# Probabilities transposed by DMA instead of TensorE, and second-half query columns multiplied tile by tile

## The reference

```
x = x + attn(layernorm(x));  x = x + ffn(layernorm(x))

qkv = (x @ w_qkv.T).reshape(B, N, 3, H, hd);  q, k, v = ...
att = softmax(einsum('bnid,bnjd->bnij', q, k) * hd**-0.5)   # over the 16 heads of one token
out = einsum('bnij,bnjd->bnid', att, v)
attn = out.transpose(0, 2, 1, 3).reshape(B, N, D) @ w_proj.T

ffn = fake_quant(relu(fake_quant(x) @ fake_quant(kernel) + fake_quant(bias)))
```

## Time and profile before

| | |
|---|---|
| three runs, us | 636.46, 634.66, 635.04; median 635.04 |
| the profiled execution, us | 635.95, with a span of 634.3 from first to last instruction |
| cores in it | 631.6 to 634.3 us, granted clock 0.990 to 0.993 |
| TensorE busy | 606.1 us (96%) |
| VectorE, ScalarE, GpSimd busy | 407.9 us (64%), 266.6 us (42%), 34.7 us (5%) |
| DMA | 103.48 MB, mean 163 GB/s |

### The profile page before, as it was taken

The page is one execution under the profiler, slowest core; times in us unless marked ns, Lnnn a source line. Parts: engine busy times, 40 slices in busy tenths (PEclk is TensorE's granted clock), DMA queues, the critical chain, the costliest instruction groups (busy, mean ns, idle before and its releaser), DMA issues.

```text
span 634.3 us, 9870 instructions; the slowest of 8 cores (631.6 to 634.3 us)
## 1 busy us (share of the span) xinstructions
PE 606.1 (96%) x3468; PEld 304.6 (48%) x3468; DVE 407.9 (64%) x685; ACT 266.6 (42%) x491; POOL 34.7 (5%) x68
## 2 busy tenths in 40 slices
PE   6768999999999999999999999999999999999993
PEld 6634444444444444444444455555555444444442
DVE  3745888777778768761001346787787654888557
ACT  2763333443333344330010465767877422653331
POOL 0000100000100100001120000000000000000000
PEclk9999999999999999999999999999999999999998
DMA  8997899889999999758996672384433494062313
GB/s 236 261 217 221 139 237 219 174 190 195 190 230 185 228 232 194 177 102 150 154 157 102 120 168 78 101 246 121 133 94 61 157 285 136 30 196 106 102 66 133
DMA packets 54114, 103.48 MB, mean 163 GB/s; under 512 B 35633, under 2 KB 35633, under 8 KB 50225
## 3 DMA queue, kind: packets, MB, share of 16 engines
q0 software_dynamic: 9216, 33.56, 33.4%
q1 hardware_dynamic: 42674, 60.90, 31.7%
q10 hardware_dynamic: 2176, 8.39, 3.9%
HBM read 111.21 MB, written 16.79 MB: 202 GB/s over the span
## 4 chain that ended last, share of the span: by engine, by line
PE 89%; DMA 6%; DVE 2%; issue 1%; SPq 1%; ACT 1%; DVEq 0%; ACTq 0%
PE pF L832 50%; PE pF L937 17%; PE pF L914 17%; DMA xbuf<-x_att 6%; PE pF L871 1%; PE pF L895 1%; PE pH L881 1%; PE pF L872 1%; SPq L219 1%; PE pF L956 1%; PE pF L850 1%; DVE cols L514 0%; DVE xr L640 0%; DVEq L214 0%; DVE xr L807 0%
## 5 line engine op out<-in xcount | busy, mean ns | idle before, releaser
L832 PE MATMUL pF<-aT,wqb 128*128 128x512 bf16 x1504 | 327.1, 379 | 5.0 <-DMA wqb<-wqkv 5.0
L832 PEld LDWEIGHTS pF<-aT,wqb 128*128 128x128 bf16 x1504 | 146.4, 98 | 179.3 <-issue 5.4
L914 PE MATMUL pF<-wpq,qT 128*128 128x512 bf16 x512 | 119.6, 379 | 0.0
L937 PE MATMUL pF<-kq,xqT 128*128 128x512 bf16 x496 | 107.2, 379 | 1.2 <-DVE xr L640 1.2
L937 PEld LDWEIGHTS pF<-kq,xqT 128*128 128x128 bf16 x496 | 48.5, 98 | 59.9 <-issue 1.7
L914 PEld LDWEIGHTS pF<-wpq,qT 128*128 128x128 bf16 x512 | 47.8, 98 | 47.2
L385 ACT ACTIVATE wkz<-wkf 128x2048 f32<-128x2048 f32 x16 | 59.1, 3691 | 21.0 <-DVE wkf L607 21.0
L395 ACT ACTIVATE Ebuf<-pF,cols 128x128 bf16<-128x128 f32 x128 | 45.4, 368 | 24.6 <-DVE cols L621 24.5
L541 DVE CAST vT<-pF 128x512 bf16<-128x512 f32 x16 | 11.0, 689 | 62.7 <-PE pF L832 62.7
L685 DVE SCALAR_TENSOR_TENSOR tt<-pF,cols,bqb 128x512 f32<-128x512 f32 x31 | 23.2, 749 | 33.0 <-PE pF L937 33.0
L320 POOL DMA_DIRECT2D wqb<-wqkv x48 | 26.0, 543 | 298.7 <-PE pF L832 244.0
(11 more groups left out here) (79 smaller groups left out, 533.4 us busy)
## 6 DMA issues: line engine op xcount, KB each, us to landing
wqb<-wqkv POOLq DMA_DIRECT2D x48, 512.0 KB, 8.1
wkf<-wk SPq DMA_DIRECT2D x16, 1024.0 KB, 8.4
xbuf<-x_att SPq DMA_DIRECT2D x8, 1024.0 KB, 19.9
kq_spill<-kqr SPq DMA_DIRECT2D x16, 512.0 KB, 5.9
wpq<-wp POOLq DMA_DIRECT2D x16, 512.0 KB, 9.6
xr<-x_res ACTq DMA_DIRECT2D x8, 1024.0 KB, 6.7
kq<-kq_spill SPq DMA_DIRECT2D x4, 2048.0 KB, 11.1
out<-xr SPq DMA_DIRECT2D x7, 1024.0 KB, 4.2
```

The lines of the kernel that those rows point to most:

```text
L832: mm = tn.matmul(pF[QBANK[j]][:, :], wqb[e % NW][:, 128 * c:128 * (c + 1)], aT[:, 8192 * h + 512 * c: 8192 * h + 512 * (c + 1)], start=(c ...
L914: mm = tn.matmul(pF[SLOTB[f % 3]][:, :], sT[:, 2048 * b + 128 * m: 2048 * b + 128 * (m + 1)], wpq[u][:, 512 * m:512 * (m + 1)], start=(m = ...
L937: mm = tn.matmul(pF[y % 4][:, :], xqT[:, 2048 * k + 128 * c: 2048 * k + 128 * (c + 1)], w[:, c, :, :], start=(c == 0), stop=(c == NC - 1))
```

## The change

The transposes of the probabilities leave TensorE and become DMA transposes on SP's queue (`e_transpose`), from `Ebuf` straight to `aTT`, so ScalarE's copy goes as well. `Ebuf` and `aTT` get three buffers each. SP's fixed list is built anew around the 32 transposes: V tile b goes after group 4b-2's transpose, the load of `kq[0]` after group 8's, layer-norm transposes 0 to 2 after groups 17, 23 and 29. In the head the second half of jobs 4 to 7 is done token tile by token tile, over the four jobs, with the transposes of tiles 5 to 7 between; tile 4's transpose comes after job 1, and none between jobs 2 and 3. Weight blocks 1 to 3 are given out one token tile earlier. SP's first FFN loads wait for the seventh normalised tile instead of job 3. ScalarE alternates strictly between normalising a tile and copying its transpose, and VectorE copies job 2 ahead of tile 6's statistics. The zeros for the warm-up matmuls get a name of their own.

```diff
--- before.py
+++ after.py
@@ -92,9 +92,10 @@
     wqb = [A(f"wqb{i}", [128, 2048], BF16, offset=180224 + 4096 * i)
            for i in range(NW)]
     Ebuf = [A(f"Ebuf{i}", [128, 512], BF16, offset=204800 + 1024 * i)
-            for i in range(2)]
-    aTT = [A(f"aTT{i}", [128, 512], BF16, offset=206848 + 1024 * i)
-           for i in range(2)]
+            for i in range(3)]
+    aTT = [A(f"aTT{i}", [128, 512], BF16, offset=207872 + 1024 * i)
+           for i in range(3)]
+    zero = A("zero", [128, 128], BF16, offset=204800)
     ident = A("ident", [128, 128], BF16, offset=210944)
     neg = A("neg", [128, 128], BF16, offset=211200)
     cols = A("cols", [128, 312], F32, offset=211456)
@@ -223,7 +224,7 @@
                     inc(sync.dma_start(ident[:, :], d_ident[:, :]), "cL", 16)
             inc(sync.dma_start(neg[:, :], d_neg[:, :]), "cN", 16)
 
-            sync.wait_ge(S_("qMM"), 4)
+            sync.wait_ge(S_("aN"), 7)
             inc(sync.dma_start(wkf[0][:, :], d_wk[0:128, :]), "kL0", 16)
             inc(sync.dma_start(wkf[1][:, :], d_wk[128:256, :]), "kL1", 16)
             sync.wait_ge(S_("qMM"), 5)
@@ -257,6 +258,15 @@
                     V8[b % 2].rearrange("p (c n) -> p c n", c=NC),
                     vT[:, 2048 * b:2048 * (b + 1)]), f"vT{b}", 16)
 
+            def e_transpose(g):
+
+                sync.wait_ge(S_("vNm"), g + 1)
+                if g >= 3:
+                    sync.wait_ge(S_("tO"), g - 2)
+                inc(sync.dma_start_transpose(
+                    aTT[g % 3].rearrange("p (j n) -> p j n", j=4),
+                    Ebuf[g % 3][:, :]), f"eT{g % 3}", 16)
+
             def l_transpose(b):
                 sync.wait_ge(S_("lQ"), 2 * b + 2)
                 inc(sync.dma_start_transpose(
@@ -279,15 +289,16 @@
                     d_out[128 * k:128 * (k + 1), :].rearrange(
                         "p (h c) -> p h c", h=2), xr_tile(k)), "oS", 16)
 
-            for b in range(5):
-                v_transpose(b)
-            kq_load(0)
-            l_transpose(0)
-            v_transpose(5)
-            v_transpose(6)
-            l_transpose(1)
-            v_transpose(7)
-            l_transpose(2)
+            v_transpose(0)
+            v_transpose(1)
+            for g in range(NG):
+                e_transpose(g)
+                if g % 4 == 2 and 2 <= g // 4 + 1 < NT:
+                    v_transpose(g // 4 + 1)
+                if g == 8:
+                    kq_load(0)
+                if g in (17, 23, 29):
+                    l_transpose((g - 17) // 6)
             sync.wait_ge(S_("tO"), NG)
             sync.wait_ge(S_("bSt"), 16)
             inc(sync.dma_start(bqb[:, :], d_bq.partition_broadcast(128)),
@@ -329,7 +340,7 @@
 
             for e in range(NE):
                 if e < 5:
-                    g.wait_ge(S_(f"xL{e + 2 if e else 1}"), 16)
+                    g.wait_ge(S_(f"xL{(1, 2, 3, 4, 6)[e]}"), 16)
                 if e >= NW:
                     g.wait_ge(S_("qMM"), JIDX[(e - NW, 1)] + 1)
                 wq_load(e)
@@ -388,11 +399,11 @@
 
             def exps(g):
                 s.wait_ge(S_("vMx"), g + 1)
-                if g >= 2:
-                    s.wait_ge(S_("tA"), g - 1)
+                if g >= 3:
+                    s.wait_ge(S_(f"eT{g % 3}"), 16 * (g // 3))
                 for j in range(4):
                     cs = slice(128 * j, 128 * (j + 1))
-                    i = s.activation(Ebuf[g % 2][:, cs], pF[3 + g % 2][:, cs],
+                    i = s.activation(Ebuf[g % 3][:, cs], pF[3 + g % 2][:, cs],
                                      AF.Exp, bias=cc(C_NM[g % 2] + j),
                                      accum_out=cc(C_DEN[g % 2] + j))
                 inc(i, "sEx")
@@ -404,12 +415,6 @@
                 inc(s.dma_start(
                     xr_tile(b), d_xres[128 * b:128 * (b + 1), :].rearrange(
                         "p (h c) -> p h c", h=2)), f"xrL{b}", 16)
-
-            def att_evac(g):
-                s.wait_ge(S_("tA"), g + 1)
-                if g >= 2:
-                    s.wait_ge(S_("tO"), g - 1)
-                inc(s.copy(aTT[g % 2][:, :], pH[g % 2][:, 0:512]), "sAT")
 
             def st_evac(g):
                 s.wait_ge(S_("tO"), g + 1)
@@ -454,17 +459,11 @@
             at_evac(0)
             norm(2)
             at_evac(1)
-            norm(3)
-            at_evac(3)
-            norm(4)
-            norm(5)
-            at_evac(4)
-            q_evac(1)
-            norm(6)
-            at_evac(5)
-            norm(7)
-            at_evac(6)
-            at_evac(7)
+            for t in range(3, NT):
+                norm(t)
+                at_evac(t)
+                if t == 4:
+                    q_evac(1)
             for j in range(3, NQ):
                 if j % 2 == 1:
                     q_evac(j)
@@ -480,8 +479,6 @@
                     exps(sl)
                 if sl < NG and sl % 4 == 3:
                     xres_load(sl // 4)
-                if 1 <= sl and sl - 1 < NG:
-                    att_evac(sl - 1)
                 b, r = (sl - L0) // LP, (sl - L0) % LP
                 if 0 <= b < NT:
                     if r < 2:
@@ -628,7 +625,7 @@
                 h = inc(v.reciprocal(cc(C_RD[g % 2], 4), cc(C_DEN[g % 2], 4)),
                         "vS")
                 wt(v, h)
-                e3 = Ebuf[g % 2].rearrange("p (j n) -> p j n", j=4)
+                e3 = Ebuf[g % 3].rearrange("p (j n) -> p j n", j=4)
                 rb = cc(C_RD[g % 2], 4).unsqueeze(2).broadcast_to([128, 4, 128])
                 inc(v.tensor_tensor(e3, e3, rb, ALU.mult), "vNm")
 
@@ -701,7 +698,7 @@
 
             inc(v.memset(cc(C_EPS), EPS), "aVar0")
             inc(v.memset(cc(C_NMG), -MAGIC), "vNmg")
-            inc(v.memset(aTT[0][:, 0:128], 0.0), "vZ")
+            inc(v.memset(zero[:, :], 0.0), "vZ")
             stats(0)
             stats(1)
             at_evac(0)
@@ -711,13 +708,13 @@
             at_evac(2, both=True)
             stats(4)
             at_evac(3)
-            stats(5)
             q_evac(0)
             at_evac(4)
+            stats(5)
+            q_evac(2)
             stats(6)
+            at_evac(5)
             stats(7)
-            at_evac(5)
-            q_evac(2)
             at_evac(6)
             at_evac(7)
             for j in range(4, NQ):
@@ -873,18 +870,8 @@
                                    start=False, stop=True)
                 inc(mm, "tS")
 
-            def a_transp(g):
-                tn.wait_ge(S_("vNm"), g + 1)
-                if g >= 2:
-                    tn.wait_ge(S_("sAT"), g - 1)
-                for j in range(4):
-                    tr = tn.transpose(pH[g % 2][:, 128 * j:128 * (j + 1)],
-                                      Ebuf[g % 2][:, 128 * j:128 * (j + 1)],
-                                      ident[:, :])
-                inc(tr, "tA")
-
             def av(g):
-                tn.wait_ge(S_("sAT"), g + 1)
+                tn.wait_ge(S_(f"eT{g % 3}"), 16 * (g // 3 + 1))
                 if g % 4 == 0:
                     tn.wait_ge(S_(f"vT{g // 4}"), 16)
                 if g >= 1:
@@ -894,7 +881,7 @@
                     c0 = 512 * (g % 4) + 128 * j
                     mm = tn.matmul(pF[2][:, cs],
                                    V8[(g // 4) % 2][:, c0:c0 + 128],
-                                   aTT[g % 2][:, cs], start=True, stop=True)
+                                   aTT[g % 3][:, cs], start=True, stop=True)
                 inc(mm, "tO")
 
             def p_part(b, u, c0, c1):
@@ -963,8 +950,8 @@
             def warm(n):
 
                 for i in range(n):
-                    tn.matmul(pF[5][:, 0:128], aTT[0][:, 0:128],
-                              aTT[0][:, 0:128], start=True, stop=True)
+                    tn.matmul(pF[5][:, 0:128], zero[:, :],
+                              zero[:, :], start=True, stop=True)
 
             tn.wait_ge(S_("vZ"), 1)
             warm(144)
@@ -977,13 +964,17 @@
             a_transpose(3)
             q_tiles(0, 0, 3, 12, NC)
             q_tiles(0, 3, 4)
-            for j in range(1, 4):
-                q_part(j, 0, NC)
-                a_transpose(3 + j)
-            a_transpose(7)
-            q_tiles(4, 0, 3)
-            q_tiles(4, 3, 4)
-            for j in range(5, NQ):
+            q_part(1, 0, NC)
+            a_transpose(4)
+            q_part(2, 0, NC)
+            q_part(3, 0, NC)
+
+            for t in range(4):
+                for e in range(HEADE):
+                    q_tiles(HEADE + e, t, t + 1)
+                    if e == 1 and t < 3:
+                        a_transpose(5 + t)
+            for j in range(2 * HEADE, NQ):
                 q_part(j, 0, NC)
 
             for sl in range(NS):
@@ -999,8 +990,6 @@
                         y_part(*YORD[sl - Y0], c0, c1)
                     elif half == 0:
                         y_last()
-                    if half == 0 and 1 <= sl <= NG:
-                        a_transp(sl - 1)
```

## The result

| | before | changed |
|---|---|---|
| runs, us | 634.66 to 636.46, median 635.11 (4) | 645.84, 648.46, 641.73, 648.49, median 647.15 |
| ratio | | 1.0164, 95% interval 1.0108 to 1.022 |
| the profiled execution | 635.95 (span 634.3) | 645.84 (span 644.2) |

The change made the kernel 1.6% slower; 628.9 was forecast, in 625 to 633. Each ratio is to the kernel before as timed beside that run (median 634.48 to 635.38 in the experiments); it is not the quotient of two medians.

The account below looks back on a forecast made before the run. The prediction took TensorE as the bound, with 89% of the chain of waits. 635.95 - 7.0 (attention) + 0.5 (stall) + 0.3 (head) = 629.75, less 0.9 for the median: 628.9 us, range 625 to 633.

Parts of the forecast that it names:

- Four transposes less per slot, -7.0: Attention: 32 slots each lose 0.22 us of TensorE transposes, 7.0 us in all, so a slot becomes 4.13.
- A landing of 2.3 us: Attention: each 128x512 DMA transpose lands in 2.3 us (bounds 1.8 and 5.3), hidden in the 6.9 to 8.2 available.
- transposes set the pace: Attention rival: with three buffers, landings above 8.8 us make slots longer than before; 648 at 10 us; chance 0.09.
- The 2 MB load, +0.5: Attention: the first FFN weight load holds group 9's transpose behind it on SP's queue; stall 0 to 0.8, taken as 0.5.
- the forecast's worst case: Attention: the stall from the 2 MB load with the next V transpose in between, 3 us at worst.
- Head, +0.3: Head: the whole rearrangement, with jobs 4 to 7 tile by tile, comes out 0.3 us slower.
- Job 3's wait: Head: TensorE's idle time before job 3 grows from 2.07 to 3.1 us.
- both waits on ScalarE: Head: TensorE waits 0.9 and 0.8 us for ScalarE's chain before the transposes of tiles 6 and 7.
- The clock: Head rival: the new 3.1 us gap brings the half clock, 3.5 us of it lose 1.7, giving 630.6; chance 0.15.
- Weights bound by shared DMA time: Head: issuing blocks 1 to 3 earlier lengthens the queue, not the rate; block 3 still arrives at 46.2.
- VectorE's lag hidden: After the head: VectorE's later FFN weight work is done at 91.1, before job 15 needs the bank at 92.9.
- The stated signs for "wrong": Slot above 4.13, TensorE idle before most attention products, PSUM-copy waits near job 15, clock 0.5 after 46, job 3 ending well before 49.

Follow-up runs that it names:

- e6: As e3, but the last quarter of the output projection's weights and the eight residual loads are constant fills instead of loads; 631.48 us, ratio 0.9942.
- e4: As e3, but the second V transpose is issued after group 1's transpose instead of before group 0's; 674.52 us, ratio 1.0599.
- e3: The changed kernel with the head of before and the first FFN weight quarter's load issued after the 32nd transpose; 649.5 us, ratio 1.0248.
- e1: The kernel before with only the head of the changed one, attention as before; 637.67 us, ratio 1.0044.
- e12: As e1, but weight blocks 1 to 3 are issued at the old token tiles; 636.69 us, ratio 1.0034.
- e9: As e3, but residual loads on SP's queue, groups 0 to 5 transposed by TensorE, kq[0] in four pieces, second layer-norm transpose after group 24; 629.6 us, ratio 0.9916.

## Why the prediction was wrong

- **Four transposes less per slot, -7.0: right.** Slot 4.12; e6 shows -6.8 in all.
- **A landing of 2.3 us: right alone, wrong in company.** This is the step that failed. It was scaled from V transposes that had the DMA engines to themselves (78% of a slice on one queue), with 5.3 as the upper bound; the changed kernel showed up to 15.3, e4 up to 33.4. Of the 32 new ones many must run beside GpSimd's weight loads (slots 1 to 4) and the residual loads (every fourth slot). The forecast counted the bytes of this traffic as nothing and never asked who else was on the DMA engines when a transpose runs. The rival "transposes set the pace" had the sign and the size (648), but named no cause and got 0.09; its condition, a landing over 8.8 us, held for a few transposes and not for all, so the loss comes in two or three large waits and not in every slot. That its number fits is luck.
- **The 2 MB load, +0.5: right for group 9, too small in all.** The stall before group 9's product came, 1.45 us on the slowest core, 0.95 and 0.45 on two others, none on five. With the 7.26 before group 11's, which the forecast's worst case put at 3, the waits before groups 9 to 11 come to 10.1 us over the eight cores. e3 takes such waits away and gains nothing, since those at the residual loads grow.
- **Head, +0.3: the waits right, the base wrong.** Job 3's wait and both waits on ScalarE came within 0.2 us of the forecast; job 8's start did too, but only since an earlier block 3 and the half clock cancel. A piece is 55.8 ns (96 of them from 63.48 to 68.84), near the 55 that the prediction states, though its own numbers, 1.05 less 0.2 over sixteen, give 53. And the forecast was set against core 5, the slowest of the profile before, whose job 8 began at 68.3; the mean over the cores was 66.5 (start of job 5 plus 10.35), against 68.4 in the changed kernel. The head costs 1.8 by that, 2.7 by e1's time.
- **The clock: it did fall,** on five of eight cores, the rival given 0.15. Its premise, that a gap of 2.1 us leaves the pace alone, was read on core 5; in the same profile job 2 of core 0 took 5.30 us after a gap of 2.04. The time is that of the slowest core, so a loss of 1.7 us on some cores can count in full: the slowest core of the changed kernel and that of e1 both have it.
- **Weights bound by shared DMA time: right** (e12). **VectorE's lag hidden: right,** no wait in jobs 8 to 89.
- The stated signs for "wrong" named TensorE idle before the attention product in most slots. It was idle before four of the 32 on the slowest core, three times for more than 1 us, and that was enough.

## What to carry to other kernels

Before work moves from an idle-free engine to DMA, list for each new transfer what other queues have in flight at that moment, not only whether its own queue is free: here transposing DMAs alone landed in 2.3 us, and the slowest beside other queues in 10 to 33. If they must be there, put everything that moves at the same time into the transposes' own queue, in order, and leave to TensorE those that would meet a queue you can't move (e9). Take the base of a forecast from all cores, since the slowest core before needn't be the slowest after.

## What the runs showed of the hardware that was not expected

- A 128x512 bfloat16 DMA transpose needs 0.58 us of the DMA engines alone (544 packets) and 1.2 us of SP's queue to issue. Beside one other queue 534 packets took 4 us (changed kernel, core 6); beside two, 976 took 20 us at 53 GB/s in sum over all queues (e4, core 6), plain transfers included.
- Giving a V transpose a later place in the same queue cost 25 us (e4 against e3), by what it then met.
- The clock: in the changed kernel gaps of 2.30 to 2.99 us before job 3 were followed by the half clock on five cores (5.07 to 5.30 us for the job), gaps of 2.09, 2.43 and 3.15 on the other three were not (3.61).
- The waits differ between cores that do the same work (span 633.3 to 644.2) and between executions (641.73 to 648.49); with all that moves beside the transposes in their own queue (e9) they are gone and the cores of e9 lie within 1.7 us.
- The Trainium skill says of a transpose next to ordinary DMAs that it "needs nothing" (DMA: Bandwidth & Descriptors, Rules for kernel authors). The row is about keeping the data right, and in that the changed kernel agrees with it; of the time it says nothing, and there the company cost 4 us for 534 packets and 20 us for 976, as above.
